# Part 2 of a two-layer block: expert projections as one sum over weighted, transposed tokens

## The reference

```python
rw = gating(h)                       # h = layernorm(x), 16 weights for each token, many of them zero
q = einsum('bte,bted->btd', rw, einsum('btc,ecd->bted', h, q_proj))   # k and v likewise, d = 64
attn = softmax(causal(q @ k.T / 8)) @ v
mixed = attn[:, :, None, :] * rw[..., None]
out = x + einsum('bted,edc->btc', mixed, o_proj)
```

## Time and profile before

| | |
|---|---|
| median of three runs | 1561.92 us |
| the profiled execution | 1562.82 us |
| its span in the trace | 1561.0 us |
| granted TensorE clock, mean | 0.976 of full speed |
| busy over the span: TensorE, VectorE, ScalarE, GpSimd | 90%, 67%, 54%, 30% |
| start of the gate stage, start of the first projection | 1163.9 us, 1199.6 us |

### The profile page before, as it was taken

The page is one execution under the profiler, slowest core; times in us unless marked ns, Lnnn a source line. Parts: engine busy times, 40 slices in busy tenths (PEclk is TensorE's granted clock), DMA queues, the critical chain, the costliest instruction groups (busy, mean ns, idle before and its releaser), DMA issues.

```text
span 1561.0 us, 55718 instructions
## 1 busy us (share of the span) xinstructions
PE 1400.3 (90%) x24918; PEld 1045.0 (67%) x24918; DVE 1047.6 (67%) x1603; ACT 847.2 (54%) x1753; POOL 467.6 (30%) x496
## 2 busy tenths in 40 slices
PE   3799999999999999999999999999963778877876
PEld 1467777777777777777777777777751455555554
DVE  5877666666866666686666668676327677777776
ACT  2346555666555565655556565565633444545553
POOL 4221323324342332334233233422322222222221
PEclk9899999999999999999999999999976899999999
DMA  4201011010110101011110101000011000000000
GB/s 115 51 16 30 23 23 37 10 43 13 33 23 23 37 10 43 13 33 24 23 35 11 43 13 33 23 23 3 3 28 28 3 8 6 8 8 7 8 8 9
DMA packets 37037, 36.43 MB, mean 23 GB/s; under 512 B 14272, under 2 KB 24256, under 8 KB 36800
## 3 DMA queue, kind: packets, MB, share of 16 engines
q1 hardware_dynamic: 35712, 31.83, 8.6%
q10 hardware_dynamic: 1088, 1.05, 0.3%
HBM read 5.33 MB, written 2.10 MB: 5 GB/s over the span
## 4 chain that ended last, share of the span: by engine, by line
PE 75%; DVE 10%; POOL 6%; issue 4%; ACT 4%; ACTq 0%; DMA 0%; DVEq 0%; POOLq 0%; SPq 0%
PE att_ps L547 30%; PE st_ps L531 15%; PE ring_ps L598 14%; PE ring_ps L585 4%; POOL sum_P L502 3%; PE qkv_ps L701 3%; POOL sum_P L505 2%; DVE part L1374 2%; DVE part_max L1171 2%; PE ring_ps L578 2%; PE ring_ps L624 2%; PE ring_ps L616 1%; ACT by_A L988 1%; DVE nm L1420 1%; PE t_ps L744 1%
## 5 line engine op out<-in xcount | busy, mean ns | idle before, releaser
L1171 DVE TENSOR_REDUCE part_max<-ring_ps 128x2 f32<-128x1024 f32 x512 | 624.0, 1224 | 329.0 <-PE ring_ps L598 319.9
L547 PEld LDWEIGHTS att_ps<-v_sb,pT 128*64 128x64 f32 x16384 | 632.6, 138 | 145.3 <-issue 28.9
L547 PE MATMUL att_ps<-v_sb,pT 128*64 128x65 f32 x16384 | 650.6, 222 | 2.4 <-issue 2.4
L864 ACT ACTIVATE pT<-st_ps 128x512 f32<-128x512 f32 x1024 | 554.5, 608 | 169.5 <-PE st_ps L531 162.9
L531 PE MATMUL st_ps<-qa,ka 98*64 98x512 f16 x2048 | 398.4, 386 | 4.4 <-issue 3.8
L598 PE MATMUL ring_ps<-ka,qa 96*64 96x512 f16 x2048 | 310.5, 383 | 9.5 <-DVE part_max L1171 5.3
L701 PE MATMUL qkv_ps<-ew_split,x2T 128*128 128x384 f16 x768 | 156.2, 335 | 25.9 <-issue 18.8
L872 ACT ACTIVATE raw_attn<-att_ps 128x260 f32<-128x260 f32 x128 | 49.6, 388 | 205.7 <-PE att_ps L547 205.7
L531 PEld LDWEIGHTS st_ps<-qa,ka 98*64 98x64 f16 x2048 | 115.3, 109 | 67.1 <-issue 14.8
L598 PEld LDWEIGHTS ring_ps<-ka,qa 96*64 96x64 f16 x2048 | 95.8, 112 | 39.4 <-DVE part_max L1171 11.7
L502 POOL TENSOR_TENSOR sum_P<-by_A 128x576 f32<-128x576 f32 x32 | 44.9, 1403 | 256.0 <-ACT by_A L988 256.0
(11 more groups left out here) (201 smaller groups left out, 1315.6 us busy)
## 6 DMA issues: line engine op xcount, KB each, us to landing
qa<-split SPq DMA_DIRECT2D x192, 64.0 KB, 2.0
ka<-split SPq DMA_DIRECT2D x180, 64.0 KB, 2.0
resid<-in_L_attn_x SPq DMA_DIRECT2D x4, 512.0 KB, 7.3
out<-yo SPq DMA_DIRECT2D x32, 64.0 KB, 1.5
qa<-shift_rows ACTq DMA_DIRECT2D x62, 4.0 KB
ka<-split ACTq DMA_DIRECT2D x12, 64.0 KB, 2.0
wkv_sb<-in_L_attn_Wkv SPq DMA_DIRECT2D x1, 512.0 KB, 5.3
ew<-in_L_ffn_q_proj SPq DMA_DIRECT2D x1, 512.0 KB, 5.8
```

The source lines that it names most:

```text
L547: mm = pe.matmul(att_ps[q0:q0 + TILE_COLS, qt * DV1:(qt + 1) * DV1], pT[:, blk % 2, kt, qt * P + q0:qt * P + q0 + TILE_COLS], v_sb[:, j % ...
L864: act.activation(pT[:, blk % 2, kt, :], st_ps[:, c % ST_BANKS, :], ACT.Exp).then_inc(exp_ok, 1)
L1171: dve.tensor_reduce(part_max[:, which % 2, 2 * quarter + m // 2, m % 2, :], pair.rearrange("p (n k) -> p n k", n=2), AX.X, ALU.max, negate ...
```

## The change

The routing weights are applied to the transposed tokens ahead of the product, and TensorE sums over the experts in PSUM:

- Once, after the gate: TensorE transposes `rw_all` (4 transposes), ScalarE copies the rows to `rw_rows`, and SyncE writes them (256 KB) to an internal tensor in device memory.
- For each tile SyncE reads 8 KB of it, the 16 rows of 128 weights, into every one of the 128 partitions (`rw_wide`, two buffers, 1 MB a transfer). The transfer of tile m waits until GpSimd is done with tile m - 2; in SyncE's list it stands behind the store of tile m - 7 and ahead of that of tile m - 6.
- The gate's ScalarE also copies the transposed normed tokens in float32 into `x2nT` (8 copies of 128x512), which lies in the memory of `xnT`; `x2T` keeps two batches only.
- For each tile, in four quarters of four experts, one iteration ahead: GpSimd multiplies (`z32`, 128x512), ScalarE rounds to float16 (`z16`, high), VectorE subtracts (`z16`, low).
- `project(m, part)` runs 12 matmuls of 192 columns, 48 in a tile, all into one bank of `qkv_ps`; the stationary operand is now `z16`, another one for each expert.
- `weighted`, `together`, `by_A`, `sum_P`, `part`, `qkv` and GpSimd's sums go. `high_parts` and `low_parts` read `qkv_ps`. `qk_ps` has a bank to itself, and three waits on `y_done`, `mx_ok` and `qkt_ok` go. The lists of TensorE, ScalarE and VectorE are put in another order.

```diff
+            sp.wait_ge(rows_sb, 1)
+            sp.dma_start(rows_out.rearrange("(b r) q -> r b q", r=P), rw_rows[:, :, :]).then_inc(rows_in_dram, 16)
+            sp.wait_ge(rows_in_dram, 16)
+            def spread_weights(m):
+                if not live(m):
+                    return
+                if m >= 2:
+                    sp.wait_ge(z_ok, QUARTERS * (m - 1))
+                sp.dma_start(rw_wide[:, m % 2, :, :].rearrange("p e q -> p (e q)"),
+                             rows_out[E * m:E * (m + 1), :].rearrange("(a e) q -> a (e q)", a=1).to_broadcast([P, E * P])).then_inc(wide_in[m % 2], 16)
+            for m in range(SPREAD_LEAD):
+                spread_weights(m)
             for tile in range(B * NT):
+                spread_weights(tile + SPREAD_LEAD)
                 sp.wait_ge(y_done, tile + 1)
...
             for m in range(B * NT):
-                pool.wait_ge(weighted_A, 2 * len(PAIRS_A) * (m + 1))
-                if m >= 2:
-                    pool.wait_ge(weighted_V, OPS_V * (m - 1))
-                pool.tensor_tensor(sum_P[:, m % 2, :, :], by_A[:, m % 2, 0:3, :], by_A[:, m % 2, 3:6, :], ALU.add).then_inc(added_P, 1)
...
+                pool.wait_ge(wide_in[m % 2], 16 * (m // 2 + 1))
+                pool.wait_ge(g_X, 2 * B)
+                for part in range(QUARTERS):
+                    if m:
+                        pool.wait_ge(z_lo, QUARTERS * (m - 1) + part + 1)
+                    pool.tensor_tensor(z32[:, part, :, :], x2nT[:, m * P:(m + 1) * P].unsqueeze(1).to_broadcast([P, E // QUARTERS, P]),
+                                       rw_wide[:, m % 2, E // QUARTERS * part:E // QUARTERS * (part + 1), :], ALU.mult).then_inc(z_ok, 1)
...
+            def project(m, part):
+                if not live(m):
+                    return
+                if part == 0 and m >= 2:
+                    pe.wait_ge(v2_ok, m - 1)
+                    pe.wait_ge(lo2, 2 * (m - 1))
+                pe.wait_ge(z_lo, QUARTERS * m + part + 1)
+                for e in range(E // QUARTERS * part, E // QUARTERS * (part + 1)):
+                    for k, (x_part, w_part) in enumerate(SPLIT_PRODUCTS):
+                        mm = pe.matmul(qkv_ps[:, m % 2, 0:3 * DE], z16[:, m % 2, x_part, e, :], ew_split[:, w_part, e, :],
+                                       start=e == 0 and k == 0, stop=e == E - 1 and k == 2)
+                if part == QUARTERS - 1:
+                    mm.then_inc(qkv_ok, 1)
...
             for m in range(B * NT + PART2_LAG):
-                outputs(m - 4)
                 project(m, 0)
                 project(m, 1)
                 qk_transposes(m - 1)
+                outputs(m - 4)
                 p_transposes(m - 2)
+                scores2(m - 1)
                 project(m, 2)
-                scores2(m - 1)
+                values2(m - 2)
+                m_transposes(m - 3)
                 project(m, 3)
-                values2(m - 2)
-                project(m, 4)
-                m_transposes(m - 3)
-                for pair in (5, 6, 7):
-                    project(m, pair)
...
-            for m in range(B * NT + PART2_LAG):
+            for m in range(-1, B * NT + PART2_LAG):
                 high_parts(m - 1)
-                weighted(m, 0)
+                high_tokens(m + 1, 0)
                 qk_copy(m - 1)
+                high_tokens(m + 1, 1)
                 p_copy(m - 2)
-                weighted(m, 2)
+                high_tokens(m + 1, 2)
                 softmax2(m - 1)
-                weighted(m, 4)
+                high_tokens(m + 1, 3)
                 m_copy(m - 3)
...
+            def low_tokens(m, part):
+                if not live(m):
+                    return
+                dve.wait_ge(z_hi, QUARTERS * m + part + 1)
+                experts = slice(E // QUARTERS * part, E // QUARTERS * (part + 1))
+                dve.tensor_tensor(z16[:, m % 2, 1, experts, :], z32[:, part, :, :], z16[:, m % 2, 0, experts, :],
+                                  ALU.subtract).then_inc(z_lo, 1)
...
-            for m in range(B * NT + PART2_LAG):
+            for m in range(-1, B * NT + PART2_LAG):
                 low_parts(m - 1)
+                low_tokens(m + 1, 0)
                 add_tokens(m - 4)
-                weighted(m, 1)
                 p_copy(m - 2)
+                low_tokens(m + 1, 1)
                 maxima2(m - 1)
-                weighted(m, 3)
+                low_tokens(m + 1, 2)
                 mixed(m - 2)
-                weighted(m, 5)
+                low_tokens(m + 1, 3)
                 m_low(m - 3)
-                weighted(m, 6)
-                weighted(m, 7)
-                together(m)
```

More of the change, by code:

```diff
@@ L684, in _ @@
             gate_logits(B - 1)
[L685 removed]
             pe.wait_ge(rw_ok, 1)
             pe.wait_ge(g_V, 2 * B)
[L689 removed]
+            pe.wait_ge(g_X, 2 * B)
+            for b in range(B):
+                mm = pe.transpose(t_ps[:, 0, b * P:(b + 1) * P], rw_all[:, b * NT:(b + 1) * NT, :].rearrange("p t e -> p (t e)"),
+                                  ident[:, :])
+            mm.then_inc(rows_ps, 1)
+            pe.wait_ge(w_lo, 2)
+            def project(m, part):
                 if not live(m):
                     return
[L692 to L704 removed]
+                if part == 0 and m >= 2:
[8 more added lines that the diff above has]
+                    mm.then_inc(qkv_ok, 1)
             def outputs(m):
@@ L977, in _, with high_tokens @@
             act.activation(gl[:, 8, :, :], gl[:, 7, :, :], ACT.Exp).then_inc(g_exp, 1)
[L979 removed]
+            act.wait_ge(rows_ps, 1)
+            act.activation(rw_rows[:, :, :], t_ps[:, 0, :].rearrange("p (b q) -> p b q", b=B), ACT.Copy).then_inc(rows_sb, 1)
+            def high_tokens(m, part):
                 if not live(m):
                     return
[L982 to L989 removed]
+                act.wait_ge(z_ok, QUARTERS * m + part + 1)
+                if part == 0 and m >= 2:
+                    act.wait_ge(qkv_ok, m - 1)
+                experts = slice(E // QUARTERS * part, E // QUARTERS * (part + 1))
+                act.activation(z16[:, m % 2, 0, experts, :], z32[:, part, :, :], ACT.Copy).then_inc(z_hi, 1)
             def qk_copy(m):
@@ L1354, in _ @@
             link(dve.tensor_tensor(rw_all[:, :, :], gl[:, 9, :, :], per_token(gs[:, 1, :]), ALU.mult), rw_ok)
-            def weighted(m, pair):
+            def low_tokens(m, part):
                 if not live(m):
                     return
-                dve.wait_ge(pair_ok, 8 * m + pair + 1)
-                for e in (2 * pair, 2 * pair + 1):
-                    n = 2 * PAIRS_V.index(pair) + e % 2
-                    into, before = CHAIN_V[n]
-                    if before is not None:
-                        dve.wait_ge(weighted_V, OPS_V * m + before + 1)
-                    elif into:
-                        dve.wait_ge(added_P, 3 * (m + 1))
-                    elif m:
-                        dve.wait_ge(weighted_V, OPS_V * m)
-                    weight = rw_all[:, m, e:e + 1]
-                    if n == 0:
-                        dve.tensor_scalar(part[:, 0, :], expert_out(m, pair, e), weight, None, ALU.mult).then_inc(weighted_V, 1)
-                    else:
-                        dve.scalar_tensor_tensor(out=part[:, into, :], in0=expert_out(m, pair, e), scalar=weight,
-                                                 in1=sum_P[:, m % 2, 0, :] if before is None else part[:, into, :],
-                                                 op0=ALU.mult, op1=ALU.add).then_inc(weighted_V, 1)
-            def together(m):
-                if not live(m):
-                    return
-                dve.wait_ge(weighted_V, OPS_V * (m + 1) - 1)
-                if m >= 2:
-                    dve.wait_ge(v2_ok, m - 1)
-                    dve.wait_ge(lo2, 2 * (m - 1))
-                dve.tensor_tensor(qkv[:, m % 2, :], part[:, 0, :], part[:, 1, :], ALU.add).then_inc(weighted_V, 1)
+                dve.wait_ge(z_hi, QUARTERS * m + part + 1)
+                experts = slice(E // QUARTERS * part, E // QUARTERS * (part + 1))
+                dve.tensor_tensor(z16[:, m % 2, 1, experts, :], z32[:, part, :, :], z16[:, m % 2, 0, experts, :],
+                                  ALU.subtract).then_inc(z_lo, 1)
             def low_parts(m):
```

91 lines of the change are left out of this document (31 added, 60 removed).

## The result

The changed kernel takes 1514.84 us (median of 4 runs, 1512.19 to 1515.58) against 1562.06 us before (4 runs): ratio 0.9696, 95% interval 0.9681 to 0.971. That is 47 us faster; 33 were forecast, and the time lies in the forecast range. The profiled execution took 1515.15 us with a span of 1513.4.

A forecast was written before the change was run, and what follows sets the result against it. Before, no engine was full and a chain of waits through GpSimd bound the kernel; afterwards VectorE's cycle with the lock would. 1562.8 - 49.6 (loop) + 14.7 (start) + 1 (clock) = 1528.9, said as 1529 us; range 1500 to 1566.

The forecast's parts named there:

- The bound: Settled loop after the change: VectorE's cycle, including a stand-still beside GpSimd, sets the tile at 9.0 us; TensorE's list needs 8.0.
- the lock: VectorE's low_tokens, both operands in SBUF, stops while a GpSimd product runs; quarter 2 loses about 0.7 us a tile.
- The size of the tile: Loop: a tile falls from 10.6 to 9.0 us, saving 31 x 1.6 = 49.6 us.
- the second bank of transposes: In VectorE's cycle: in half the tiles p_copy waits 0.1 to 0.5 us for it; with hops 8.7 becomes 9.0.
- TensorE's floor: Loop: TensorE's own work per tile, 8.0 us, of which 3.84 is projection matmuls.
- The start: Before the first tile: gate copies, transposes, write, first spread and first products add 14.7 us, lower clock another 1.
- The tail: Emptying after the last tiles: unchanged, since its tiles project nothing.
- Taking the link out: Chain of waits in every tile: GpSimd's three sums, 2.75 us, stand in it once; the change removes them.
- Rival A: Loop: the lock costs nothing and TensorE becomes the bound, 8.3 us a tile, 1505 us; chance 0.15.
- Rival B: Loop: the lock hits more than once or ScalarE's chain comes last, 9.8 us a tile, 1553 us; chance 0.12.
- Rival C: Spread transfer lands past 7 us, products slide into VectorE's subtractions, 11.9 us a tile, 1619 us; chance 0.10.
- Rival D: TensorE's projection matmuls stall on weight loads, step 0.15 instead of 0.08, floor 11.4 us, 1603 us; chance 0.03.

The follow-up runs named there:

- experiment 1: Changed kernel with GpSimd multiplying only 32 of each expert's 128 tokens; ratio 0.9567 to the kernel before, 8.24 us a settled tile.
- experiment 2: Changed kernel with two of the three float16 products in the projections, 32 matmuls a tile instead of 48; ratio 0.9702 to the kernel before.
- 12: Changed kernel with both GpSimd's products cut to 32 of 128 tokens and two of three float16 projection products; ratio 0.9523 to the kernel before.
- experiments 4: Changed kernel with VectorE's quarters 2 and 3 of low_tokens moved behind mixed and m_low; ratio 0.9717 to the kernel before, 8.83 us a tile.
- experiment 5: Changed kernel with each spread transfer preceded by a second 1 MB one that nothing reads, GpSimd waiting for both; ratio 0.976 to the kernel before.
- Experiment 6: Kernel before, with VectorE's second last step of part taking zeros instead of GpSimd's sum, without waiting; ratio 0.9875 to the kernel before.
- experiments 3: Changed kernel with outputs(m - 4) back at the head of TensorE's list, ahead of project(m, 0); ratio 1.0112 to the kernel before.
- 8: Changed kernel with TensorE's list as outputs, qk_transposes, p_transposes, scores2, then three projection quarters; ratio 0.992 to the kernel before.
- 9: Changed kernel with TensorE's outputs, qk_transposes, p_transposes and scores2 first, then one projection quarter ahead of values2; ratio 0.9731 to the kernel before.
- experiment 10: Changed kernel with tile 0's spread as four 256 KB transfers, each with its own semaphore; 1512.65 us, ratio 0.9689 to the kernel before.

## Why the prediction was right, point by point

- **The bound.** Right: VectorE's cycle with the lock sets the tile, TensorE's list lies close below. Experiments 1, 2 and 12 show the three levels. The readings that were forecast came nearly as said: quarter 2 long (1.36 to 1.79 in the four shortest tiles, where 1.2 to 1.4 was said), the others 0.68, products 1.27 just behind a subtraction, projection steps of 0.08, clock 1.00, transfers 5.1 us (5.5).
- **The size of the tile**, 9.0 forecast, 8.57 measured: this term makes 0.43 x 31 = 13.4 us of the 14 by which the forecast was too slow. Term by term over eight tiles: the path from the start of `qk_transposes` to `add_tokens` takes 1.71 us, where transposes, `outputs` and hop had been summed to 1.9 (the transposes took 0.17, `outputs` 1.50, the hop 0.04 and not 0.2); the lock 0.60 and not 0.7; the waits for the second bank of transposes, with hops, 0.23 and not the 0.3 added for them; reciprocal and `mixed` 1.45 and not 1.5. Smaller terms nearly cancel, which gives the settled 8.64. The mean over all tiles is 8.57, since the first two took 7.6 and 6.7 us.
- **TensorE's floor**, 8.0 forecast; experiment 1 shows only that it is at most 8.24.
- **The start**, +14.7 and +1 forecast, +12.5 measured. That it was 3.2 too dear and the tail, put at nothing, cost 2.7 nearly cancels, which is luck. The gate lost 1.4 us instead of 3.3 (`rw_all` starts at 1200.20 against 1198.83). The transfers took 2.3 and 4.2 us instead of 3 and 5.5:

```profile
1202.10 0.60 ACT L989 ACTIVATE rw_rows<-t_ps 128x512 f32<-128x512 f32 x1 [6.59 <-PE t_ps L702]
...
1202.72 0.38 SPq L350 DMA_DIRECT2D rows_of_weights<-rw_rows  x1
1205.03 30.14 SPq L359 DMA_DIRECT2D rw_wide<-rows_of_weights  x6
1209.33 27.18 POOL L516 TENSOR_TENSOR z<-xnT,rw_wide 128x512 f32<-128x512 f32 x17 [15.04 <-DMA rw_wide<-rows_of_weights]
```

  From the first product to the first `qs` went 13.1 us instead of 11.0. The turns of subtraction and product took 1.67 us each, where 1.95 had been reckoned, and the projection of tile 0 ended by 1218.9, within 9.6 us; but ScalarE's `high_parts(0)` stands behind the four quarters of tile 1 in its list. I had costed the work and not that place.
- **The tail**, called unchanged, lost 2.7 us. `outputs` now stands ahead of the last tile's scores, 1.3 us, of which 0.2 is won back just before it. Some 1.5 us came from the clock, most of it here (changed, then before, then the changed kernel's window):

```profile
1496.91 2.63 PE L732 MATMUL rest_ps<-eow_split,mxT 128*128 128x128 f16 x24 [2.38 <-DVE mxT L1430]
```
```profile
1546.21 1.51 PE L716 MATMUL rest_ps<-eow_split,mxT 128*128 128x128 f16 x24 [2.38 <-DVE mxT L1441]
```
```profile
1496.00:1500.00 4.00, 3.09 (x28) 3.09 (x29) 1.14 (x3) 0.02 (x1) 0.00 (x0) 0.63 0.00 0
```

  The same 24 matmuls behind the same idle 2.4 us took 1.51 us before and 2.63 after, at a granted clock of 0.63 in the window (0.50 from 1498 to 1500 us). Nor does the new order alone bring this on: experiments 4 and 5 have the changed kernel's order at this place and the same idle time, and took 1.51, while 1, 2 and 12 took 1.96 to 2.74. What decides it is open. "The tail's tiles project nothing" was true and not enough: the order of what they do had changed, which costs 1.1 us.
- **Taking the link out.** The prediction read the chain of waits as "the change takes that link out". Experiment 6 prices the link alone at 0.4 us a tile. The sum didn't rest on it, since it was made from the new cycle.
- **Rival A** (TensorE the bound, 1505) named a level that lay only some 0.4 us a tile below the measured one; experiment 2 rules it out as the cause. **Rival B** (9.8 us a tile) didn't come: the lock fell once a tile. **Rival C** has its point about right and its price ten times too high at 7.2 us (experiment 5). **Rival D**: the step is 0.08, and TensorE has no stall of that kind.

## What to carry to other kernels

When engines meet in every tile, find the cycle: add the steps of one engine and only those pieces of the others that it waits for. An engine that is busy 98% of the time can still be worth nothing (experiment 2), and a link on the chain of waits can be worth a seventh of its length (experiment 6: 0.4 of 2.75 us). Where VectorE works on two operands in SBUF beside GpSimd, ask what runs beside every product of GpSimd, here for 1.3 us behind each subtraction; and when a piece is moved in one engine's list, walk the whole circle again, over its end to its head, before believing the gain (experiments 3, 4, 8 and 9 failed just there).

## What the runs showed of the hardware

GpSimd stands still for VectorE as well, which no row of before had shown. In the first tiles, where both always have work, GpSimd's products took 1.71 us instead of 1.27, and start at intervals of 1.67 us:

```profile
1209.33 1.26 POOL L516 TENSOR_TENSOR z<-xnT,rw_wide 128x512 f32<-128x512 f32 x1 [15.04 <-DMA rw_wide<-rows_of_weights]
...
1211.78 1.71 POOL L516 TENSOR_TENSOR z<-xnT,rw_wide 128x512 f32<-128x512 f32 x1
...
1213.45 1.71 POOL L516 TENSOR_TENSOR z<-xnT,rw_wide 128x512 f32<-128x512 f32 x1
```

This is the direction that the Trainium skill's page "SBUF — State Buffer", section "Who interferes with whom", adds; the trace agrees. In the settled loop it cost nothing, since a product waits for its subtraction anyway (mean 1273 ns from 1260 to 1480 us).

1 MB read out of the same 8 KB for all 128 partitions landed in 5.1 us (4.2 to 6.4), sooner than the 7.4 of the 512 KB load, which was queued behind others; the first 256 KB of it still took 3.1 (experiment 10).
